# Last layer of a three-layer graph attention kernel: slots dealt anew to the engines, scores earlier in a period, own rows of the second layer weighted by ScalarE, last bias at other places

## The chip, the cores and the metric

The kernel runs on one core of one Trainium2 chip, as one launch. A core has TensorE (PE, matrix multiply, with its weight loads shown apart as PEld), VectorE (DVE), ScalarE (ACT), GpSimd (POOL) and SyncE (SP, which here only issues DMAs). Each engine takes its own instructions in order, and semaphores tie them together. The metric is the device time in microseconds (us).

## The reference, cut to what matters

The graph has 3125 nodes of 256 features and 53125 edges, sorted by destination. Three attention layers run one after the other (4 heads, 1 head, 8 heads). The first two are one residual block with a layer norm behind it, the third is the other:

```python
def gat_layer(x, src, dst, W, a_src, a_dst, bias, heads, out_ch):      # layers 1 and 2; in both, every
    xW = (x @ W).reshape(n, heads, out_ch)                             # node also has an edge to itself
    e = leaky_relu(sum(xW * a_src)[src] + sum(xW * a_dst)[dst], 0.2)
    w = exp(e - segment_max(e, dst)[dst])
    alpha = w / segment_sum(w, dst)[dst]
    return segment_sum(xW[src] * alpha[:, :, None], dst).reshape(n, heads * out_ch) + bias
...
    # layer 3, h = x @ W.T
    enc = relu(edge_attr @ edge_W.T + edge_b).reshape(-1, H, D)
    alpha = einsum(h[src], a_src) + einsum(h[dst], a_dst) + sum(enc * h[dst], axis=-1)
    # then leaky_relu, softmax over the edges of a destination, weighted sum of h[src], + bias
...
x = layernorm(x + L0(x)); x = layernorm(x + L1(x))
```

## The kernel before, in words

**Tiling.** The nodes lie in 25 blocks of 128 partitions (`nodes`). The edges are cut into slots of 128 edges that all end in one block, 440 slots, handled in `K` = 40 batches of `B` = 11 slots. A layer (index l = 0, 1, 2) first projects all blocks and writes a table of rows to memory, then runs 40 periods, one for each batch. In a period, slot s of the batch t is weighted (each of its 128 gathered rows times its edge weights, in place in `rows`), multiplied on PE with a matrix of zeros and ones that adds the rows of one destination (`sum_slot`, L1658), and the product is added to the sums of its block by DVE (`add`, L826). The sums stand in only two PSUM banks in the last layer, so the matmul of slot s waits for the add of slot s - 2.

**Who weights a slot.** `OWNER` is a string for each layer: V for DVE (one TENSOR_TENSOR, L815), A for ACT (one ACTIVATE for each head, L1414, 8 in the last layer), P for POOL (one TENSOR_TENSOR, L1237). DVE and ACT do it `LEAD[l]` positions ahead of the slot's matmul, two in the last layer: at position s they weight slot s + 2 of t, or, from position 9 on, slot 0 or 1 of the next batch.

**Beside it, each engine prepares the batches to come.** `n1`, `n2`, `n3` are the batches one, two, three later; `AT[l]` is a table that gives the position at which each small step is written. In the last layer DVE runs, in this order: `rescale` (L807) at the start of a period, `links` at 2, `finish_tops` (L779 to L787) at 5, `hot` (L707) at 7, `scores` of n2 (L717, L722) at 8, `tops` (L739, L745) and `tops2` (L753) at 10. Between them stand the dot products of encoded edge features with destination rows, in six groups a batch (`dot` L835, `dot2` L844), each after PE's `encode` (L1670, L1677) and ACT's `encode` (L1422). Batch k + 3 is encoded in period k, so the last three periods have none. ACT runs beside its weightings and encodings: `hotT` (L1366) at 2 and 5, `link` and `rescale` (L1382 to L1393) at 3, `expw` (L1399) at 6, `weights` (L1407, which hands out the edge weights of n1) at 8, the copy of scores (L1373) at 9. PE runs the matmuls that feed all of these. A semaphore `w` counts `weights`, `wp` the transpose that it copies, `fac` the factor of `rescale`, `ad` the lookup that `scores` reduces.

**POOL** in a period weights its slots of t and then issues the 11 row gathers of batch t + 3 by indirect DMA (L1225), in three groups of 4, 4 and 3. A group waits until PE has used the same buffers in batch t, that is for the matmuls of slots 0 to 3, 4 to 7 and 8 to 10.

**Ends of a layer.** A node's own row (its edge to itself) is not gathered. In layers 0 and 1 POOL weights it (`self_mul`, L1242) and adds the sums to it (`self_add`, L1249), block by block, in four runs of blocks (`READY`) as soon as the sums of a run are complete and DVE has computed their denominators (`self_weights`, L571 to L576). Then DVE forms the residual (L611), statistics and norm, PE and ACT project. ACT's `deviation` (L1332, a square root) stands first in its work for the last layer. In the last layer the bias of the block (L851) is added to all 25 blocks: three ahead of the first scores, 11 in each of the periods with three and with two batches left.

## Time and profile before

| what | value |
|---|---|
| median of 3 runs | 2139.15 us (2136.64 to 2141.73) |
| profiled execution, its time | 2139.67 us |
| profiled execution, its span | 2137.9 us |
| around the span (time less span) | 1.8 us |
| last layer, its 40 periods | 1420.7 to about 2117 us of the span |
| busy over the span | PE 76%, DVE 76%, POOL 72%, ACT 57% |
| granted TensorE clock, mean | 0.854 of full speed |

The span is the time from the first to the last instruction on the core. The table is read by stages, since the four engines are bound by different things in each: the busy shares over the whole span hide that in the last layer one engine is at work nearly all the time. A line number (L826) is that of the kernel printed above.

### The profile page before, as it was taken

Reading aid. Unit: us, or ns where it says so; the run is one execution under the profiler, and the core shown is the slowest. Engines: PE = TensorE matmul, PEld = TensorE weight load, DVE = VectorE, ACT = ScalarE, POOL = GpSimd, SP = SyncE. Lnnn points to the kernel's source line nnn. Section 1 sums busy time; section 2 is a strip of 40 time slices with the busy share of each in tenths; the row PEclk is TensorE's granted clock in tenths of the full one; section 3 lists DMA queues with packets and bytes.
Section 4 is the critical chain, followed back from the end, with each engine's and each line's share of the span. In section 5 each row is a group of like instructions: output and inputs, shape, how many; then the busy total and the mean of one; then the engine's idle time right before and its main releaser. Section 6 shows DMA issues by size and latency. Waiting matters only on the chain. (4 is left out here: it accounts for less than half of the span.)

```text
span 2137.9 us, 42617 instructions
## 1 busy us (share of the span) xinstructions
PE 1634.7 (76%) x9240; PEld 1035.0 (48%) x9240; DVE 1618.8 (76%) x4473; ACT 1219.4 (57%) x4310; POOL 1547.9 (72%) x1714
## 2 busy tenths in 40 slices
PE   6378778877774667777778776688998999989984
PEld 5245545555552434444445444345555555555552
DVE  5567777777678556666666667869999999999998
ACT  4257766676663445554555553546666666666655
POOL 3767777777778277777777777567788877878863
PEclk9577877787887778888887797879999999999995
DMA  6744554445640344444444641243444444444421
GB/s 197 177 136 141 141 142 141 137 142 157 187 121 30 95 128 136 135 136 135 136 129 134 197 122 39 89 125 112 126 137 131 127 125 127 130 131 132 134 75 60
DMA packets 131326, 274.35 MB, mean 128 GB/s; under 512 B 40389, under 2 KB 65968, under 8 KB 131061
## 3 DMA queue, kind: packets, MB, share of 16 engines
q0 software_dynamic: 64128, 181.33, 30.8%
q1 hardware_dynamic: 62259, 86.45, 13.3%
q10 hardware_dynamic: 4699, 3.86, 0.6%
q8 instruction: 92, 1.51, 0.3%
q14 instruction: 148, 1.21, 0.2%
HBM read 255.34 MB, written 17.20 MB: 127 GB/s over the span
## 5 line engine op out<-in xcount | busy, mean ns | idle before, releaser
L1225 POOL DMA_INDIRECT rows<-table,index_all x1320 | 1280.7, 970 | 478.6 <-issue 351.6
L1658 PE MATMUL bank<-rows,onehot 128*128 128x264 f32 (+1 forms) x2640 | 957.5, 473 | 167.4 <-ACT rows L1414 113.2
L826 DVE TENSOR_TENSOR sums<-sums,bank 128x264 f32 (+1 forms) x1320 | 554.8, 420 | 234.6 <-PE bank L1658 111.7
L1414 ACT ACTIVATE rows<-rows,wgt 128x65 f32<-128x65 f32 (+2 forms) x2480 | 664.1, 352 | 0.1
L1658 PEld LDWEIGHTS bank<-rows,onehot 128*128 128x128 f32 x2640 | 496.6, 222 | 339.5 <-ACT rows L1414 155.3
L1422 ACT ACTIVATE prod<-bank 128x512 f32<-128x512 f32 x240 | 134.9, 562 | 204.3 <-PE bank L1670 181.4
L1366 ACT CAST onehot<-bank 128x768 f32<-128x768 bf16 x240 | 175.3, 740 | 128.5 <-PE bank L1581 128.0
L1677 PE MATMUL bank<-late,onehotT 128*128 x1320 | 193.2, 282 | 0.7 <-DVE prod L835 0.7
L1373 ACT COPY scoreT<-bank 44x256 f32<-44x256 f32 (+2 forms) x120 | 39.6, 330 | 263.2 <-PE bank L1611 210.5
L835 DVE TENSOR_TENSOR prod<-prod,bank 128x512 f32<-128x512 f32 x240 | 151.7, 632 | 11.1 <-PE bank L1677 6.6
L1581 PE MATMUL bank<-identb,onehotT 128*128 128x128 bf16 x1320 | 143.6, 258 | 11.7 <-DVE onehotT L707 6.9
L844 DVE TENSOR_REDUCE dots<-prod 128x16 f32<-128x512 f32 x240 | 151.4, 631 | 0.5
L815 DVE TENSOR_TENSOR rows<-rows,wgt 128x260 f32<-128x260 f32 (+2 forms) x320 | 149.2, 467 | 0.7 <-ACT wgt L1407 0.6
L1677 PEld LDWEIGHTS bank<-late,onehotT 128*128 128x128 bf16 x1320 | 112.2, 100 | 62.4 <-issue 45.8
L1237 POOL TENSOR_TENSOR rows<-rows,wgt 128x264 f32<-128x264 f32 x200 | 129.1, 672 | 6.0 <-ACT wgt L1407 5.4
L1581 PEld LDWEIGHTS bank<-identb,onehotT 128*128 128x128 bf16 x1320 | 108.3, 117 | 44.2 <-issue 23.8
L1611 PE MATMUL bank<-ident,score 128*44 128x128 f32 (+1 forms) x160 | 39.1, 336 | 116.7 <-DVE score L729 113.9
L1594 PE MATMUL bank<-dtab,onehotT 128*128 x1320 | 104.3, 178 | 10.9 <-issue 10.3
L1594 PEld LDWEIGHTS bank<-dtab,onehotT 128*128 128x128 bf16 x1320 | 86.1, 97 | 43.1 <-issue 12.3
L1670 PE MATMUL bank<-edgew,late 30*128 30x256 bf16 x440 | 91.2, 280 | 9.2 <-DVE onehotT L707 8.5
L1564 PE MATMUL bank<-wts,rows 128*128 128x264 f32 (+2 forms) x300 | 87.0, 416 | 2.6 <-ACT rows L1313 2.6
L1399 ACT ACTIVATE expT<-expT 44x256 f32<-44x256 f32 (+2 forms) x120 | 45.5, 379 | 72.3 <-DVE expT L787 68.8
(200 smaller groups left out, 1787.6 us busy)
## 6 DMA issues: line engine op xcount, KB each, us to landing
locb<-loc_d SPq DMA_DIRECT2D x120, 352.0 KB, 3.7
rows<-table,index_all POOLq DMA_INDIRECT x1320
flags<-flags_d SPq DMA_DIRECT2D x520, 27.5 KB
table<-rows SPq DMA_DIRECT2D x25, 136.0 KB, 1.8
table<-rows SPq DMA_DIRECT2D x25, 134.0 KB, 3.1
late<-table SPq DMA_DIRECT2D x1, 3300.0 KB, 17.2
table<-rows SPq DMA_DIRECT2D x25, 129.5 KB, 2.0
late<-table SPq DMA_DIRECT2D x1, 3212.5 KB, 16.6
```

Of the source, the lines that this page charges most:

```text
L815: done(v.tensor_tensor(r, r, w.to_broadcast([P, H, n]), ALU.mult), "mulv")
L826: done(v.tensor_tensor(a, a, sum_bank(l, t, s)[:, 0:VV], ALU.add), "add")
L835: done(v.tensor_tensor(prod[:, i % 2, 0:w], prod[:, i % 2, 0:w], ps_hdst[i % 2][:, 0:w], ALU.mult), "prod")
L844: done(v.tensor_reduce(dots[:, t.u, :, lo:hi].rearrange("p h s -> p s h"), prod[:, i % 2, 0:(hi - lo) * D].rearrange("p (s h c) -> p s h c ...
L1225: g.indirect_dma_start(out=rows[:, t.u, s, 0:ROW[l]], out_offset=None, in_=table[l], in_offset=bass.IndirectOffsetOnAxis(ap=index_all[:, t ...
L1366: done(a.copy(onehot[:, t.u, lo:hi, :].rearrange("p s e -> p (s e)"), ps_hotb[l][g][:, 0:(hi - lo) * P]), "hotT")
L1414: i = a.activation(r, r, ACT.Copy, scale=wgt[:, t.u, h * B + s:h * B + s + 1])
L1422: done(a.activation(prod[:, i % 2, 0:w], ps_enc[:, 0:w], ACT.Relu), "enc")
L1581: r = m.transpose(ps_hotb[l][g][:, (s - lo) * P:(s - lo + 1) * P], onehotT[:, t.u, s * P:(s + 1) * P], identb[:, :])
L1594: r = m.matmul(ps_e[:, AD + s * 24:AD + (s + 1) * 24], onehotT[:, t.u, s * P:(s + 1) * P], dtab3[:, bass.ds(b, 1), :, :].rearrange("p a i ...
L1658: done(m.matmul(sum_bank(l, t, s)[:, 0:VV], onehot[:, t.u, s, :], rows[:, t.u, s, 0:VV], start=True, stop=True), "agg")
L1677: r = m.matmul(ps_hdst[i % 2][:, (s - lo) * D:(s - lo + 1) * D], onehotT[:, t.u, s * P:(s + 1) * P], hnode3[:, bass.ds(b, 1), j, :].rearra ...
```

## The change

It has five parts. (1) `OWNER` of the last layer: DVE has slots 0 and 2 (before 0, 1, 3), ACT 1, 3, 5, 7, 9 (before 2, 5, 8), POOL 4, 6, 8, 10 (before 4, 6, 7, 9, 10). (2) In the last layer `scores` of n2 stands at position 5 for DVE and its transpose at 8 for PE (before 8 and 9), the second `hot` of PE at 5 and `hotT` of ACT at 6 (before 4 and 5); DVE's scores no longer wait for `w` of n1 but for its `fac`, and PE's transpose of the weights of n1 waits for those scores. (3) Own rows of layer 1 are weighted by ACT (`self_scale`), one a slot in the last period and 14 in a row behind it. (4) POOL only adds there. (5) Of the 25 bias additions of the last layer, 11 stand ahead of the first period, 11 in the period with three left, 3 in the next.

```diff
-OWNER = ("AVAAVAAVAAV", "VAAAAAAAAAA", "VVAVPAPPAPP")
+OWNER = ("AVAAVAAVAAV", "VAAAAAAAAAA", "VAVAPAPAPAP")
...
+BIASED = 11
...
-    dict(links=2, finish=5, mask=10, scores=8, tops=10, hot=7, load=7,
-         link=3, exp=6, weights=8, hotT=(2, 5), copy=9,
-         endsT=1, cols=4, weightsT=7, hotP=(1, 4), adst=3, scoresT=9),
+    dict(links=2, finish=5, mask=10, scores=5, tops=10, hot=7, load=7,
+         link=3, exp=6, weights=8, hotT=(2, 6), copy=9,
+         endsT=1, cols=4, weightsT=7, hotP=(1, 5), adst=3, scoresT=8),
...
                     need(dve, "scT", kk)
                     need(dve, "ad", kk + 1)
-                    need(dve, "w", kk)
+                    if l == 2 and t.k > 1:
+                        need(dve, "w", kk - 1)
+                        need(dve, "fac", kk)
+                    else:
+                        need(dve, "w", kk)
...
-                        if l == 2 and left in (2, 3) and BLOCKS - 2 * B + (3 - left) * B + s < BLOCKS:
-                            bias_add(BLOCKS - 2 * B + (3 - left) * B + s)
+                        if l == 2 and left in (2, 3) and BIASED + (3 - left) * B + s < BLOCKS:
+                            bias_add(BIASED + (3 - left) * B + s)
...
                     dots_of(t0, *range(G))
-                    for b in range(BLOCKS - 2 * B):
+                    for b in range(0, 5):
                         bias_add(b)
-                    for f in (scores, tops, tops2):
-                        f(t0)
-                    dots_of(t1, 0, 1)
+                    scores(t0)
+                    for b in range(5, 7):
+                        bias_add(b)
+                    tops(t0)
+                    tops2(t0)
+                    dots_of(t1, 0)
+                    for b in range(7, 9):
+                        bias_add(b)
+                    dots_of(t1, 1)
                     links(t0)
+                    for b in range(9, BIASED):
+                        bias_add(b)
...
                     for b in READY[i]:
-                        self_mul(b)
-                        if b > READY[i][0]:
-                            self_add(b - 1)
-                    self_add(READY[i][-1])
+                        if l == 0:
+                            self_mul(b)
+                            if b > READY[i][0]:
+                                self_add(b - 1)
+                        else:
+                            self_add(b)
+                    if l == 0:
+                        self_add(READY[i][-1])
...
+                        if l == 1 and left == 1:
+                            self_scale(s)
+
+                def self_scale(b):
+
+                    for i, r in enumerate(READY):
+                        if b == r[0]:
+                            need(act, "selfq", NR + i + 1)
+                    if b == 0:
+                        act.wait_ge(s_self[1], 16)
+                    done(a.activation(selfs[1][:, b, 0:D], selfs[1][:, b, 0:D], ACT.Copy, scale=qz[:, 0, b, 0:1]), "selfx")
...
                 batches(act, period)
+                if l == 1:
+                    for b in range(B, BLOCKS):
+                        self_scale(b)
...
                     need_apart(pe, ("exp", kk + 1), ("w", kk))
+                    if l == 2 and 0 < t.k < K - 1:
+                        need(pe, "sc1", kk + 2)
```

Where it moves instructions, the engines' programs read as follows.

DVE from position 10 of one period to position 1 of the next, in the steady part of the last layer, before (L815 weights a slot, L807 starts a period, L826 adds a slot):

```order
L815 TENSOR_TENSOR rows<-rows,wgt 128x264 [waits ev_w]
L835 TENSOR_TENSOR prod<-prod,bank 128x256 [waits ev_encp,ev_enc]
L826 ISA [waits ev_add,ev_agg]
L826 TENSOR_TENSOR sums<-sums,bank 128x264
L753 SCALAR_TENSOR_TENSOR top<-flags,top 88x128 [waits ev_endp,ev_topf]
L844 TENSOR_REDUCE dots<-prod 128x8 [waits ev_prod]
L805 ISA [waits ev_w,ev_add,ev_fac,ev_ad]
L807 TENSOR_TENSOR sums<-sums,bank 128x264
L826 ISA [waits ev_resc,ev_agg]
L826 TENSOR_TENSOR sums<-sums,bank 128x264
L815 TENSOR_TENSOR rows<-rows,wgt 128x264 [waits ev_w]
L835 TENSOR_TENSOR prod<-prod,bank 128x512 [waits ev_encp,ev_enc]
```

and in the changed kernel (its lines are some five further down: L820 for L815, L812 for L807, L831 for L826):

```order
L840 TENSOR_TENSOR prod<-prod,bank 128x256 [waits ev_encp,ev_enc]
L831 ISA [waits ev_add,ev_agg]
L831 TENSOR_TENSOR sums<-sums,bank 128x264
L758 SCALAR_TENSOR_TENSOR top<-flags,top 88x128 [waits ev_endp,ev_topf]
L849 TENSOR_REDUCE dots<-prod 128x8 [waits ev_prod]
L810 ISA [waits ev_w,ev_add,ev_fac,ev_ad]
L812 TENSOR_TENSOR sums<-sums,bank 128x264
L820 TENSOR_TENSOR rows<-rows,wgt 128x264 [waits ev_w]
L831 ISA [waits ev_resc,ev_agg]
L831 TENSOR_TENSOR sums<-sums,bank 128x264
L840 TENSOR_TENSOR prod<-prod,bank 128x512 [waits ev_encp,ev_enc]
```

The weighting at position 10 is gone, and the one at position 1 stands ahead of the period's first add, between that add and the rescale that it waits for.

ACT from position 3 to position 0 of the next period, in the same part, before (L1422 encodes, L1414 weights a slot, L1366 is `hotT`, L1399 the exponential, L1407 hands out the weights, L1373 copies the scores):

```order
L1414 ACTIVATE rows<-rows,wgt 128x33 x8
L1422 ACTIVATE prod<-bank 128x512
L1366 CAST onehot<-bank 128x640
L1399 ACTIVATE expT<-expT 88x128
L1422 ACTIVATE prod<-bank 128x512
L1414 ACTIVATE rows<-rows,wgt 128x33 x8
L1407 COPY wgt<-bank 128x88
L1422 ACTIVATE prod<-bank 128x512
L1373 COPY scoreT<-bank 88x128
L1422 ACTIVATE prod<-bank 128x256
L1422 ACTIVATE prod<-bank 128x512
```

and in the changed kernel (some 17 lines further down: L1431 for L1414, L1439 for L1422):

```order
L1431 ACTIVATE rows<-rows,wgt 128x33 x8
L1439 ACTIVATE prod<-bank 128x512
L1431 ACTIVATE rows<-rows,wgt 128x33 x8
L1416 ACTIVATE expT<-expT 88x128
L1439 ACTIVATE prod<-bank 128x512
L1383 CAST onehot<-bank 128x640
L1431 ACTIVATE rows<-rows,wgt 128x33 x8
L1424 COPY wgt<-bank 128x88
L1439 ACTIVATE prod<-bank 128x512
L1390 COPY scoreT<-bank 88x128
L1439 ACTIVATE prod<-bank 128x256
L1431 ACTIVATE rows<-rows,wgt 128x33 x8
```

One weighting of eight ACTIVATEs (slot 7) now stands between the encode at position 4 and the exponential, one (slot 1 of the next batch) between the encode at 9 and the next period's first; the cast of `hotT` moved behind the encode at 6.

ACT at the end of layer 1, where its last weightings are followed by the square root of the layer norm, before:

```order
L1407 COPY wgt<-bank 128x11
L1414 ACTIVATE rows<-rows,wgt 128x257 x12
L1332 ACT_TABLE_LOAD
L1332 ACTIVATE rstd<-meanvar,eps 128x2 x2
L1313 COPY rows<-bank 128x256
```

and in the changed kernel, from the last of its weightings on (L1474 is `self_scale`; seven more stand between weightings ahead of this piece):

```order
L1431 ACTIVATE rows<-rows,wgt 128x257
L1474 ACTIVATE late<-late,qzr 128x256
L1431 ACTIVATE rows<-rows,wgt 128x257
L1474 ACTIVATE late<-late,qzr 128x256 x17
L1349 ACT_TABLE_LOAD
L1349 ACTIVATE rstd<-meanvar,eps 128x2 x2
```

The table load and the first square roots now stand behind the weighting of the last own row.

## Rows read from the trace of the kernel before

**Rows 1.** Windows, steady periods: length, busy us by engine, PEclk, DMA share, GB/s.
```profile
1482.70:2049.10 566.40, 510.42 (x3401) 317.23 (x3400) 533.59 (x1288) 368.52 (x1289) 452.50 (x529) 1.00 0.45 129
```
**Rows 2.** Timeline of DVE: starts of period 1 and of the third last.
```profile
1447.52 0.42 DVE L807 TENSOR_TENSOR sums<-sums,bank 128x264 f32 x1
...
2066.62 0.41 DVE L807 TENSOR_TENSOR sums<-sums,bank 128x264 f32 x1
```
**Rows 3.** Timeline of DVE, one period: start us, us, instruction [idle before <-releaser].
```profile
1604.03 0.42 DVE L807 TENSOR_TENSOR sums<-sums,bank 128x264 f32 x1
1604.65 0.43 DVE L826 TENSOR_TENSOR sums<-sums,bank 128x264 f32 x1 [0.21 <-DVE sums L807]
1605.00 0.73 DVE L815 TENSOR_TENSOR rows<-rows,wgt 128x264 f32<-128x264 f32 x1
1605.65 0.68 DVE L835 TENSOR_TENSOR prod<-prod,bank 128x512 f32<-128x512 f32 x1
...
1615.83 0.42 DVE L717 TENSOR_REDUCE adsum<-bank 128x88 f32<-128x264 f32 x1
...
1619.44 0.40 DVE L815 TENSOR_TENSOR rows<-rows,wgt 128x264 f32<-128x264 f32 x1
1619.76 0.41 DVE L835 TENSOR_TENSOR prod<-prod,bank 128x256 f32<-128x256 f32 x1
...
1621.08 0.41 DVE L807 TENSOR_TENSOR sums<-sums,bank 128x264 f32 x1
```
**Rows 4.** Timeline of POOL, the same period: weightings, then first gathers of two groups.
```profile
1605.42 3.17 POOL L1237 TENSOR_TENSOR rows<-rows,wgt 128x264 f32<-128x264 f32 x5
...
1608.87 0.98 POOL L1225 DMA_INDIRECT rows<-table,index_all  x1 [0.27 <-PE bank L1658]
...
1613.99 0.95 POOL L1225 DMA_INDIRECT rows<-table,index_all  x1 [0.38 <-PE bank L1658]
```
**Rows 5.** Timeline of ACT, the same period: what it waits for.
```profile
1606.27 0.60 ACT L1422 ACTIVATE prod<-bank 128x512 f32<-128x512 f32 x1 [1.14 <-PE bank L1670]
...
1610.96 0.69 ACT L1366 CAST onehot<-bank 128x640 f32<-128x640 bf16 x1
1611.76 0.31 ACT L1399 ACTIVATE expT<-expT 88x128 f32<-88x128 f32 x1
1612.44 0.60 ACT L1422 ACTIVATE prod<-bank 128x512 f32<-128x512 f32 x1 [0.37 <-PE bank L1670]
1612.93 1.80 ACT L1414 ACTIVATE rows<-rows,wgt 128x33 f32<-128x33 f32 x8
1614.63 0.21 ACT L1407 COPY wgt<-bank 128x88 f32<-128x88 f32 x1
1615.85 0.60 ACT L1422 ACTIVATE prod<-bank 128x512 f32<-128x512 f32 x1 [1.01 <-issue]
1617.15 0.26 ACT L1373 COPY scoreT<-bank 88x128 f32<-88x128 f32 x1 [0.70 <-issue]
...
1619.89 0.60 ACT L1422 ACTIVATE prod<-bank 128x512 f32<-128x512 f32 x1 [1.70 <-PE bank L1670]
```
**Rows 6.** Timeline, end of layer 1: POOL, ACT and DVE.
```profile
1296.91 1.23 POOL L1242 TENSOR_TENSOR late<-late,qzr 128x256 f32<-128x256 f32 x2 [12.21 <-DVE qzr L571]
...
1300.71 4.92 ACT L1414 ACTIVATE rows<-rows,wgt 128x257 f32<-128x257 f32 x12
1310.34 1.28 ACT L1332 ACT_TABLE_LOAD   x1 [4.71 <-DVE meanvar L552]
...
1321.50 0.28 DVE L571 SCALAR_TENSOR_TENSOR qzr<-sums 128x5 f32<-128x5 f32 x1
...
1322.72 0.17 DVE L559 RECIPROCAL rstd<-rstd 128x2 f32<-128x2 f32 x1
```
**Rows 7.** Timeline of DVE, ahead of the first period of the last layer.
```profile
1392.37 1.08 DVE L851 TENSOR_TENSOR nodes<-nodes,bias 128x256 f32<-128x256 f32 x3
...
1396.03 0.31 DVE L722 TENSOR_TENSOR score<-rows,adsum 128x88 f32<-128x88 f32 x1 [2.23 <-DMA rows<-table,index_all]
```

More of the change, by code:

```diff
@@ L283, in gat_kernel @@
             "h1 h2 h3 "
-            "selfq selfz selfr selfm selfa e5 e6 e7 ex e8 "
+            "selfq selfz selfr selfm selfx selfa e5 e6 e7 ex e8 "
             "self2 sum stat aggr std rst shf scl norm norm2").split()
@@ L1245, in self_add @@
                 def self_add(b, l=l):
-                    need(pool, "selfm", l * BLOCKS + b + 1)
+                    need(pool, ("selfm", "selfx")[l], b + 1)
                     t = own(l, b)
@@ L1298, in _ @@
             fetch(1)
-            seeded(act, "link hotT scp rrise rscale exp w mula enc yT tval ex h2 std norm2")
+            seeded(act, "link hotT scp rrise rscale exp w mula enc yT tval ex h2 std norm2 selfx")
             for l in range(3):
```

## The prediction

> **What bounds the kernel now.** I read the windows of the busy engines over a stretch of the last layer first, then the timeline of one period there, engine by engine, and then the two ends of the layer. In the steady stretch DVE is busy 533.6 of 566.4 us, which is 94%, PE 90%, POOL 80%, ACT 65%, at a granted clock of 1.00 [rows 1]. POOL's 80% deceives: the 0.27 to 0.30 us ahead of each gather is not counted as busy but is spent all the same [rows 4]. One period lasts 17.05 us, from 1604.03 to 1621.08 [rows 3], and the 36 periods from 1447.52 to 2066.62 take 619.1 us, 17.20 each [rows 2], so disturbed ones add 0.15 on average. In the clean period DVE has one wait of 0.21 us for its own rescale [rows 3] and goes from instruction to instruction otherwise. POOL goes round in the same 17.05 us: 3.17 us of weightings, then 11 gathers, and its wait before the second group is 0.38 us where 0.30 is there anyway, so only about 0.08 us is slack [rows 4]. Two engines are thus full, DVE and POOL; ACT has some 6 us idle in a period (17.2 less 65%), nearly all of it ahead of encodings and the copy of scores: 1.14, 0.37, 1.01, 0.70, 1.70 [rows 5].
>
> **DVE in a period.** It loses the weighting at position 10, which takes 0.32 us from its start to the next one's, and the one at position 1, which takes 0.65 [rows 3]. It gets one at position 0, between the rescale and the first add, where now 0.62 us pass with 0.21 of them idle [rows 3]. Rescale and weighting follow each other at some 0.34, so the first add would start at 0.68 instead of 0.62: 0.06 more. Sum: -0.65 - 0.32 + 0.06 = -0.91, so 16.14 us. This counts on the new weighting taking the short time (0.40 to the end), not the long one (0.73). The long one starts at 1605.00 and POOL's weightings at 1605.42; the other ones on DVE, away from those, take 0.40 [rows 3, 4]. At position 0 it would run from about 1604.37 and be over before POOL starts. The other end of the range is that it stays at 0.65: 16.14 + 0.31 = 16.45.
>
> Here the Trainium skill has a rule (SBUF — State Buffer, section "Who interferes with whom"): a VectorE instruction with two SBUF inputs and a GpSimd one that reads SBUF exclude each other, and the later one blocks until the first ends. The trace shows the slowdown in that pair but not that order: the DVE instruction was first by 0.42 us and was still the long one. Taken to the letter, its 0.31 us would have another cause and stay, and DVE's sum would be 16.45 instead of 16.14, which is the end of the range that the rows gave too.
>
> **POOL in a period.** Five weightings of 3.17 us become four, -0.63; with the 0.08 of slack gone the loop is 17.05 - 0.08 - 0.63 = 16.34 us [rows 4]. That is more than DVE's 16.14, so POOL is the next bound. Its gathers are released by PE's matmuls of slots 3, 7 and 10, which now also wait for ACT.
>
> **ACT in a period.** A weighted slot is eight ACTIVATEs of 1.70 us from start to the next instruction [rows 5], and it gets two more: +3.4 us. I let the idle time carry them. Slot 1 of the next batch stands ahead of the first encoding of the period, where ACT idles 1.70 us: it fits. Slot 7 stands ahead of the exponential in the place of the cast of 0.69 us, so the exponential comes 1.70 - 0.69 = 1.0 us later than at 1611.76, the encoding behind it (0.37 idle) 0.7 later, and the weights (1614.63) 1.3 later, since slot 9 and the cast stand ahead of them as well; the waits behind, 1.01 and 0.70, take that up [rows 5]. Who waits for the late ones: PE's transpose of the weights, with the matmuls of slots 7 and 8 queued behind it, for the exponential; DVE's weighting of slot 0 of the next batch at position 9 for the weights. Before, the scores at position 8 waited for these weights as well; now they stand at 5 (L717, 0.42 [rows 3]) and wait only for the factor, which is why the delay doesn't reach them. Their own time is unchanged and the lookups and gathered rows that they need are there earlier. The later cast and the earlier transposes of PE are moved within its queue, at no cost as long as PE's 10% idle covers them [rows 1]; the cost if it doesn't is the transpose's delay itself, up to 1.0 us a period. Total ACT: 65% of 17.05 is 11.1, with 3.4 it is 14.5 of 16.34. I take 0.1 us a period for waits that this tightness brings, between 0 and the 0.91 that would eat DVE's gain.
>
> A rule of the Trainium skill speaks against the change (ScalarE: Activation LUTs, section "Rules for kernel authors"): multiplications belong on VectorE, not ScalarE. The rows agree on the price, 1.70 us on ACT against 0.32 to 0.65 on DVE and 0.63 on POOL. If the engine's time were what counts, 2 x 1.70 x 36 = 122 us would be lost; what counts is whether it was idle, and the sum above needs only that.
>
> **Steady part.** Period 16.34 + 0.15 (disturbances as before) + 0.1 = 16.6 against 17.20: -0.6, times 36 = **-21.6 us**. The ends: 16.34 with nothing added, -0.86 x 36 = -31; no gain, 0.
>
> **The first period and what lies ahead.** Eight more bias additions of some 0.36 us (1.08 us for three) stand in DVE's waits ahead of the first period; the one for gathered rows alone is 2.23 us for the first four of them [rows 7]. Free; 8 x 0.36 = 2.9 if none of it were. But ACT weights slot 1 of batch 0 (1.70) ahead of its last two encodings where DVE took 0.4: I take +0.8, between 0 and 1.7, less 0.4 inside the first period, where two weightings of DVE go as well: +0.4.
>
> **The last periods.** With three batches left DVE loses the same two weightings, -0.9. With two left it also loses eight bias additions, 8 x 0.36 = 2.9, part of which waits for PE will swallow: -2.3 (between 0 and -2.9), to which the weightings add nothing that I count.
>
> **End of layer 1.** POOL loses 25 weightings of some 0.6 us (1.23 for two) [rows 6], 15 us in all, which are now ACTIVATEs of about 0.41 (4.92 us for 12 of nearly that shape [rows 6]). POOL wasn't waited for there. But ACT's first square root, with its table load, moves behind the last own row: it needs the denominators of the last run, which begin at 1321.50, so 0.3 + 5 x 0.41 + 1.28 + 0.29 = 3.9 us later, at 1325.4, where DVE reads it at 1322.72 [rows 6]: +2.7. Against it, DVE's two-input instructions from 1297 to 1328 run beside a POOL that is busy half as long; nine residuals and the denominators there could gain 1 to 3 us. I take +0.6, between -2 and +3.
>
> **Sum.** -21.6 + 0.4 - 0.9 - 2.3 + 0.6 = -23.8. The profiled execution took 2139.67 us (span 2137.9 and 1.8 around it): 2115.9; the median of the runs is 0.5 lower, so **2115.4 us**.
>
> **The rivals.** (a) *ACT becomes the pacing engine*, half covered: the late exponential and weights hold up the transpose on PE or the weighting at position 9 on DVE by some 0.35 us in each period. For it: they come 1.0 and 1.3 us late and the waits meant to absorb that are 2.1 us in all; against: PE had been standing idle for ACT in just that part. Period 16.95, -0.25 x 36 = -9, less 2.2 for the ends: 2128. (b) *The waits of ACT don't shrink*: an encoding waits for a matmul that follows slots weighted by ACT itself, so idle time may travel along with the work. If the 1.14, 0.37, 1.01 and 0.70 stayed [rows 5], the period would be 11.1 + 3.4 + 3.2 = 17.7, +0.5 x 36 = +18, less 2.2: 2155, slower. It decides from 2.7 us of kept waits a period (17.2 - 14.5). Against it: those waits are for PE matmuls that themselves hang on DVE's adds, and an engine that comes later meets them done. (c) *POOL alone sets the pace*, without the 0.1 and with fewer disturbances: -31 - 2.2 = 2106. (d) *DVE's weighting stays long* (the rule above taken to the letter): 16.45 + 0.25 = 16.7, -0.5 x 36 = -18, less 2.2: 2119.5, within the forecast's own range. (e) *It moves nothing*: DVE's gain eaten where POOL and PE release each other; then only the ends, 2137.
>
> **How the numbers follow.** Forecast with (d), 2107 to 2122: 62%, of which 12% are (d). (a), 2122 to 2133: 18%. (c), under 2107: 8%. (e): 4%. (b): 8%. The range from 2106 to 2131 leaves out (b), (e) and the outer parts of (a) and (c), some 18%. A measurement of this kernel tells about 0.2% (4.3 us) from no change: faster by more 89%, within it 4%, slower 7%.
>
> **What would show it.** Right: starts of the rescale 16.4 to 16.6 us apart; five groups of eight ACTIVATEs in a period of ACT, and its wait ahead of the first encoding gone; the DVE weighting behind the rescale at 0.4 us; POOL's loop without waits beyond 0.30; scores without a wait; the reading of the first square root at about 1323 to 1326. Wrong: DVE waiting at the product of the fourth group or at position 9 for ACT (a); ACT's waits ahead of encodings as long as before and PE waiting for rows of ACT more than now (b); the new weighting at 0.7 (d).

## The result

The changed kernel took 2128.5 us (median of 20 runs, 2116.8 to 2138.4) against 2140.9 us of the kernel before (median of 20 runs beside it): a ratio of 0.9939, interval 0.9925 to 0.9952. It is faster by 12 us where 24 were forecast. 2128.5 lies within the range on record (2106 to 2131), but at the number of rival (a), 2128, and not near the forecast of 2115. The profiled execution took 2125.35 us against 2139.67: 14.3 us less.

The starts of the rescale (now L812) say where. Before the last layer's first period the two traces stand at the same place (1420.73 before, 1420.84 after). The first period is 1.4 us shorter, the 36 steady ones 9.1 us together (619.1 to 610.0, that is 16.94 each in place of 17.20), the one with three batches left 1.3, the one with two left 2.3, what follows 0.4. So the steady part gave 9.1 us where 21.6 were forecast, and the ends together gave 5.2 us where 2.2 were forecast: the gap lies in the steady part alone, and is 12.5 us there. First the windows of the steady part of the changed kernel (columns as in [rows 1]) and, from the timelines of DVE, POOL and ACT, one of its short periods:

```profile
1482.80:2039.65 556.85, 523.77 (x3401) 332.21 (x3399) 514.38 (x1255) 463.45 (x1817) 435.67 (x495) 0.97 0.48 131
```

```profile
1701.68 0.42 DVE L812 TENSOR_TENSOR sums<-sums,bank 128x264 f32 x1
1702.02 0.42 DVE L820 TENSOR_TENSOR rows<-rows,wgt 128x264 f32<-128x264 f32 x1
1702.36 0.42 DVE L831 TENSOR_TENSOR sums<-sums,bank 128x264 f32 x1
...
1707.66 0.43 DVE L831 TENSOR_TENSOR sums<-sums,bank 128x264 f32 x1 [0.24 <-PE bank L1691]
...
1717.97 0.42 DVE L812 TENSOR_TENSOR sums<-sums,bank 128x264 f32 x1
```

```profile
1702.10 1.16 POOL L1238 DMA_INDIRECT rows<-table,index_all  x1 [0.30 <-issue]
1703.56 0.95 POOL L1238 DMA_INDIRECT rows<-table,index_all  x1 [0.30 <-issue]
1704.53 2.41 POOL L1250 TENSOR_TENSOR rows<-rows,wgt 128x264 f32<-128x264 f32 x4
...
1712.13 0.95 POOL L1238 DMA_INDIRECT rows<-table,index_all  x1 [0.30 <-issue]
```

```profile
1703.97 0.60 ACT L1439 ACTIVATE prod<-bank 128x512 f32<-128x512 f32 x1 [1.05 <-PE bank L1703]
...
1707.87 0.60 ACT L1439 ACTIVATE prod<-bank 128x512 f32<-128x512 f32 x1 [0.26 <-PE bank L1703]
...
1713.14 0.60 ACT L1439 ACTIVATE prod<-bank 128x512 f32<-128x512 f32 x1
...
1716.95 0.60 ACT L1439 ACTIVATE prod<-bank 128x512 f32<-128x512 f32 x1 [0.49 <-PE bank L1703]
```

This period takes 16.29 us and is the one that was worked out: the weighting behind the rescale takes 0.42, as forecast, and not the 0.73 of [rows 3]; four weightings on POOL take 2.41 in place of 3.17; POOL never stands for more than the 0.30 or 0.31 ahead of each gather and so is the bound, at 16.29 where the sum had said 16.34. ACT is 83% busy (463.45 of 556.85), and its waits have shrunk: the 1.14 of [rows 5] is 1.05, the 1.70 is 0.49, the 1.01 is gone. But the windows show a granted clock of 0.97 where [rows 1] have 1.00, and only some of the periods look like this one: 23 of the 36 take 16.3 to 16.7 us, the other 13 take 17.6 to 18.6, about 17.8 most of them.

One of the long ones runs from 1601.67 to 1619.43 (17.76 us). Windows of one microsecond in it, and then the timelines of PE, POOL and DVE:

```profile
1606.50:1607.50 1.00, 1.00 (x8) 0.63 (x7) 0.96 (x2) 1.00 (x6) 0.84 (x2) 1.00 0.00 0
1607.50:1608.50 1.00, 1.00 (x7) 0.59 (x7) 0.76 (x3) 0.69 (x3) 0.69 (x2) 0.68 0.00 0
1608.50:1609.50 1.00, 1.00 (x9) 0.80 (x8) 0.70 (x3) 1.00 (x7) 0.82 (x1) 0.50 0.50 139
...
1610.50:1611.50 1.00, 1.00 (x4) 0.38 (x3) 0.81 (x3) 0.00 (x0) 0.70 (x2) 0.62 0.57 151
1611.50:1612.50 1.00, 1.00 (x10) 0.73 (x10) 1.00 (x3) 0.61 (x2) 0.32 (x1) 1.00 0.61 200
```

```profile
1604.52 1.14 PE L1625 MATMUL bank<-dtab,onehotT 128*128 x11
1605.61 0.68 PE L1691 MATMUL bank<-rows,onehot 128*128 128x264 f32 x2
1606.22 0.47 PE L1662 MATMUL bank<-ones,linkrow 1*88 1x1 f32 x4
1606.55 0.36 PE L1671 MATMUL bank<-scale,carry 2*128 2x8 f32 x2
...
1607.81 1.45 PE L1710 MATMUL bank<-late,onehotT 128*128 x6
1609.06 0.74 PE L1612 MATMUL bank<-identb,onehotT 128*128 128x128 bf16 x5
1609.59 1.94 PE L1691 MATMUL bank<-rows,onehot 128*128 128x264 f32 x4
```

```profile
1613.44 0.94 POOL L1238 DMA_INDIRECT rows<-table,index_all  x1 [1.63 <-PE bank L1691]
```

```profile
1614.32 0.43 DVE L831 TENSOR_TENSOR sums<-sums,bank 128x264 f32 x1 [0.92 <-issue]
```

The clock granted to PE goes from its upper level (2.4 GHz) to the lower (1.2 GHz) at about 1608 and comes back at about 1611. In between the six matmuls of L1710 take 1.45 us instead of 0.83, and four of the sums' 1.94 instead of 1.11. POOL's second group of gathers, released by the sum of slot 7, waits 1.63 instead of 0.30, DVE's next add waits 0.92, and the period ends 1.47 us late (17.76 less 16.29). PE wasn't idle in the 4 us before the fall: the rows show it busy all through, but with the work that stands at positions 3 and 4, part of which is narrow, that is, has few columns for each matmul (eleven matmuls of 24 columns in L1625, then columns of 1 and of 8 in L1662 and L1671). The change took five transposes of 128 columns (L1612, the second group of `hot`) out of just that stretch. By the granted clock, the 36 steady periods of the changed kernel hold 13 stretches at the lower level, some 45 us in all. Twelve are of this sort: they begin 5.3 to 6.6 us into a period, with no wait of PE in the 3 us ahead of them. The first of the 13 is another sort: it begins at the end of the first period, behind waits of PE of 1.3 us together. The kernel before holds one such stretch, of 3 us, 6.4 us into its period.

### The profile page after: what moved, and what is told of

Its sections match the earlier page's. It is cut to its first block and busy times, and to the rows that moved or that the text cites. A ratio compares the mean times of both kernels' runs of the same rounds, so it can differ in the third digit from the quotient of the medians.

```text
span 2123.5 us, 43220 instructions
## 1 busy us (share of the span) xinstructions
PE 1636.8 (77%) x9240; PEld 1044.7 (49%) x9240; DVE 1592.1 (75%) x4433; ACT 1345.7 (63%) x4975; POOL 1507.5 (71%) x1649
## 3 DMA queue, kind: packets, MB, share of 16 engines
q14 instruction: 152, 1.25, 0.2%
HBM read 255.34 MB, written 17.20 MB: 128 GB/s over the span
## 5 line engine op out<-in xcount | busy, mean ns | idle before, releaser
L1431 ACT ACTIVATE rows<-rows,wgt 128x33 f32<-128x33 f32 (+2 forms) x3120 | 809.0, 344 | 0.2
L831 DVE TENSOR_TENSOR sums<-sums,bank 128x264 f32 (+1 forms) x1320 | 554.8, 420 | 239.4 <-PE bank L1691 134.3
L1439 ACT ACTIVATE prod<-bank 128x512 f32<-128x512 f32 x240 | 134.2, 559 | 124.5 <-PE bank L1703 116.2
L1710 PE MATMUL bank<-late,onehotT 128*128 x1320 | 198.9, 288 | 0.4 <-DVE prod L840 0.4
L1612 PE MATMUL bank<-identb,onehotT 128*128 128x128 bf16 x1320 | 145.0, 259 | 11.6 <-DVE onehotT L708 6.5
L1710 PEld LDWEIGHTS bank<-late,onehotT 128*128 128x128 bf16 x1320 | 114.1, 101 | 63.8 <-issue 45.3
L1612 PEld LDWEIGHTS bank<-identb,onehotT 128*128 128x128 bf16 x1320 | 113.0, 119 | 45.0 <-issue 24.3
L820 DVE TENSOR_TENSOR rows<-rows,wgt 128x260 f32<-128x260 f32 (+2 forms) x280 | 120.7, 431 | 0.7 <-ACT wgt L1424 0.6
L1625 PE MATMUL bank<-dtab,onehotT 128*128 x1320 | 104.5, 178 | 11.0 <-issue 10.0
L1625 PEld LDWEIGHTS bank<-dtab,onehotT 128*128 128x128 bf16 x1320 | 86.2, 97 | 43.7 <-issue 13.3
L1250 POOL TENSOR_TENSOR rows<-rows,wgt 128x264 f32<-128x264 f32 x160 | 98.3, 649 | 4.7 <-ACT wgt L1424 4.1
L1642 PEld LDWEIGHTS bank<-ident,score 128*44 128x44 f32 (+1 forms) x160 | 10.6, 104 | 155.8 <-DVE score L734 152.7
## 6 DMA issues: line engine op xcount, KB each, us to landing
late<-table SPq DMA_DIRECT2D x1, 3212.5 KB, 17.8
```

The source lines that it names most:

```text
L831: done(v.tensor_tensor(a, a, sum_bank(l, t, s)[:, 0:VV], ALU.add), "add")
L1431: i = a.activation(r, r, ACT.Copy, scale=wgt[:, t.u, h * B + s:h * B + s + 1])
L1439: done(a.activation(prod[:, i % 2, 0:w], ps_enc[:, 0:w], ACT.Relu), "enc")
L1612: r = m.transpose(ps_hotb[l][g][:, (s - lo) * P:(s - lo + 1) * P], onehotT[:, t.u, s * P:(s + 1) * P], identb[:, :])
L1625: r = m.matmul(ps_e[:, AD + s * 24:AD + (s + 1) * 24], onehotT[:, t.u, s * P:(s + 1) * P], dtab3[:, bass.ds(b, 1), :, :].rearrange("p a i ...
L1710: r = m.matmul(ps_hdst[i % 2][:, (s - lo) * D:(s - lo + 1) * D], onehotT[:, t.u, s * P:(s + 1) * P], hnode3[:, bass.ds(b, 1), j, :].rearra ...
```

## The experiments

Two theories stood against each other. **Theory 1**: the moved transposes leave a stretch of PE too thin, and the clock falls there. **Theory 2**: the shorter period alone brings the falls. In two of the four groups of runs, among them the first, everything waited longer: the kernel before took 2556 and 2579 us where it takes 2140. In the kernel before with only the transposes moved, a gather still took 970 ns there and an add 421 in place of 420, but the steady periods were 19.5 to 23.1 us and the clock in them 0.88. The groups are told apart below by the time of the kernel before. Ratios are compared inside a group, or between the two groups in which the kernel before took 2140 (2140.4 in that of the control, 2139.8 in the other). The changed kernel itself was not run in the groups at 2556 and 2579.

**The changed kernel again**, as a control (kernel before 2140):

> The changed kernel as it is, as a control beside the four runs ahead, in which the kernel before took 2556 us where it had taken 2140: PE stood for 1 to 4 us at a time in the middle of a period, for something that the profile doesn't name, and periods were 20.0 to 21.9 us. If those waits hold the periods whatever the owners, the changed kernel is within 0.3% of the kernel before here; if its gain is independent of them, the ratio is 0.994 as in the first comparison. Theory 1 (moved transposes) wants it above e1_hot_back, 0.9877, by 0.005 or more; theory 2 wants the two within 0.002.

2124.5 us, ratio 0.9934 (0.9914 to 0.9954). The trace shows 13 stretches at the lower clock again, some 45 us in all, the same twelve and one, and 610.2 us for the 36 periods, nearly to the decimal what the first trace had. Many of them come some 34 us apart, one in every second period (1468, 1502, 1536, 1570, 1605), which is a short and a long period together. The ratio is 0.0057 above that of the kernel of the next section in the group at 2556, as theory 1 wanted, but that comparison crosses into a group where everything waited, and shows nothing.

**The transposes back at position 4:**

```diff
-         endsT=1, cols=4, weightsT=7, hotP=(1, 5), adst=3, scoresT=8),
+         endsT=1, cols=4, weightsT=7, hotP=(1, 4), adst=3, scoresT=8),
```

> The changed kernel with one number set back: PE's second group of five transposes of the last layer (hot, slots 6 to 10) again at position 4 of the period, where it stood before, in place of 5. The changed kernel showed 11 stretches of some 3 us with the granted clock at 0.5 in the steady part, each following the narrow matmuls (24 columns) of positions 3 and 4, and each costing its period about 1.45 us. Theory 1, the moved transposes opened that gap: the stretches go, all periods are 16.3 to 16.4, and the time is 10 to 16 us below the changed kernel (2113 to 2119). Theory 2, the shorter period alone brings them, wherever the transposes stand: 8 to 14 of them stay and the time is within 3 us of the changed kernel's 2128.

> The same kernel as e1_hot_back (the changed kernel, PE's second group of five transposes of the last layer at position 4 again), repeated because in the first group of runs everything waited longer, the kernel before as well. Theory 1 (the moved transposes open a gap in PE's work, in which the clock falls): the stretches at 0.5 in the steady part go from 10 or so to at most 3, periods are 16.3 to 16.4, and the ratio to the kernel before is 0.986 to 0.989. Theory 2 (the shorter period alone brings them): 8 to 14 of them stay and the ratio is 0.993 to 0.995, that of the changed kernel.

In the first group (before 2556) 2525.7, ratio 0.9877 (0.9859 to 0.9895), which says nothing of the theories without the changed kernel beside it. Repeated (before 2140): 2120.6 us, ratio 0.9909 (0.9889 to 0.9929), neither the 0.986 to 0.989 of theory 1 nor the 0.993 and more of theory 2. The trace resolves it: the stretches go from 13 to 4 (three behind the narrow work, and the one at the end of the first period), as theory 1 wants, but the periods without one now average 16.69 us, not 16.42. In the timelines of DVE and POOL:

```profile
1672.09 0.43 DVE L831 TENSOR_TENSOR sums<-sums,bank 128x264 f32 x1 [0.84 <-PE bank L1691]
```

```profile
1676.27 1.15 POOL L1238 DMA_INDIRECT rows<-table,index_all  x1 [0.63 <-PE bank L1691]
```

In the changed kernel the same batch (its period of 16.69 us from 1668.70) has these instead:

```profile
1675.08 0.43 DVE L831 TENSOR_TENSOR sums<-sums,bank 128x264 f32 x1 [0.60 <-PE bank L1691]
```

```profile
1679.26 1.15 POOL L1238 DMA_INDIRECT rows<-table,index_all  x1 [0.40 <-PE bank L1691]
```

The waits are 0.24 and 0.23 us shorter there, and so is the period (16.69 against 16.92). In most other batches DVE's wait is 0.48 against 0.24. At position 4 the transposes delay the sum that DVE's next add waits for, and with it the slot 7 on which POOL waits. There POOL's wait is longer by less than 0.1 us, but its gather then starts beside DVE's `hot` (L708) and takes 1.15 us in place of 0.95: 26 such gathers in the 36 periods, against 2 in the control. Moving them away, as the change does, gains 0.27 us a period on average (10 us in 36) and costs nine falls. By the lengths of the periods, the 13 falls of the control cost 19 us and the four here 4.5, so the falls cost more than the place gains, and the difference is the 4.7 us between 610.2 and 605.4 us for the 36 periods.

**The same move alone, in the kernel before:**

```diff
-    dict(links=2, finish=5, mask=10, scores=8, tops=10, hot=7, load=7,
-         link=3, exp=6, weights=8, hotT=(2, 5), copy=9,
-         endsT=1, cols=4, weightsT=7, hotP=(1, 4), adst=3, scoresT=9),
+    dict(links=2, finish=5, mask=10, scores=8, tops=10, hot=7, load=7,
+         link=3, exp=6, weights=8, hotT=(2, 6), copy=9,
+         endsT=1, cols=4, weightsT=7, hotP=(1, 5), adst=3, scoresT=9),
```

> The kernel before with only PE's second group of transposes moved from position 4 to 5 and the cast behind it on ACT from 5 to 6; owners of the weightings, scores, own rows and biases as before. Theory 1 (the moved transposes open the gap in PE's wide work): several stretches at clock 0.5 in the steady part, up to one in each third period, and the time 5 to 20 us above the kernel before. Theory 2 (only the shorter period brings them): at most one or two such stretches, period 17.0 to 17.2, and the time within 3 us of the kernel before.

> The same kernel as e2_hot_alone (the kernel before with only those transposes and the cast behind them one position later), repeated for the same reason. Theory 1: several stretches at clock 0.5 in the steady part, the ratio to the kernel before 1.002 to 1.01. Theory 2: at most two of them, ratio 0.999 to 1.001. The disturbed group of runs gave 0.9993.

First group: ratio 0.9993 (0.9981 to 1.0004). Repeated (before 2140): 2144.3 us, ratio 1.0016 (1.0004 to 1.0028), three stretches against one, and 625.1 us for the 36 periods against 619.1:

```profile
1446.45:2071.56 625.11, 562.56 (x3706) 350.60 (x3704) 582.23 (x1404) 402.49 (x1412) 487.57 (x573) 0.99 0.46 126
```

The sign is that of theory 1, the number of falls nearer to theory 2. So the place of the transposes does it only in part; at a period of 17.1 us they bring two more falls, at 16.3 nine. Two more falls rest on one trace of each kernel. What else in the change brings falls, the shorter period or the other moves on PE, was not taken apart.

**Work added in the thin stretch of the changed kernel:**

```diff
                         r = m.matmul(ps_e[:, AD + s * 24:AD + (s + 1) * 24], onehotT[:, t.u, s * P:(s + 1) * P],
...
                                      start=True, stop=True)
+                        if l == 2 and s % 2:
+                            m.matmul(ps_e[:, QT:QT + 8 * B], identb[:, :], identb[:, 0:8 * B], start=True, stop=True)
                     done(r, "ad")
```

> The changed kernel with work added: behind every second of the 11 narrow matmuls (24 columns) of position 3 in the last layer PE does one more matmul, of 88 columns in bf16, into unused columns, five a period, some 0.2 us of PE in sum by the matmul rates of the trace; nobody reads them. Theory 1 (the clock falls because PE's work in positions 3 and 4 is thin): fewer stretches at 0.5, fewer than 5 of the 11, and the time 5 to 15 us below the changed kernel in spite of the added work. Rival (the falls have to do with something else, such as waits of PE in the whole period): as many stretches as without, and the time 0 to 7 us above the changed kernel.

> The same kernel as e4_filler (the changed kernel with five more matmuls of 88 columns a period among the narrow ones of position 3), repeated for the same reason. If the clock falls because PE's work is thin there: at most 4 stretches at 0.5 in the steady part, periods of 16.3 to 16.5, ratio to the kernel before 0.985 to 0.989, below the changed kernel's 0.993. If the falls come from elsewhere: 8 or more, ratio 0.993 to 0.997.

First group: 2511.7, ratio 0.983 (0.9814 to 0.9847). Repeated (before 2140): **2110.7 us, ratio 0.9859** (0.9839 to 0.988), better than both kernels. Windows over the same 36 periods, of the changed kernel's control, of the transposes at 4, and of this one:

```profile
1442.87:2053.04 610.17, 573.15 (x3710) 363.10 (x3708) 560.89 (x1369) 506.99 (x1989) 472.34 (x536) 0.96 0.47 129
```

```profile
1446.50:2051.93 605.43, 561.77 (x3707) 351.46 (x3704) 560.40 (x1369) 506.35 (x1989) 476.93 (x536) 0.99 0.48 130
```

```profile
1443.66:2037.33 593.67, 556.75 (x3890) 355.72 (x3888) 559.56 (x1369) 505.65 (x1989) 471.79 (x536) 1.00 0.49 132
```

PE does 180 matmuls more and is busy 16.4 us less. DVE, ACT and POOL are busy for the same time in the first and the third to within 1.4 us, and the clock is 1.00: one stretch is left, at the start. The 36 periods take 593.7 us, 16.5 less than in the control, with 12 stretches fewer: 1.4 us each. This is the run that settles what held the gain back: nothing but PE's own work at position 3 was changed, the falls behind the narrow work went, and the steady part is 25.4 us shorter than before where 21.6 had been forecast.

PE's idle time doesn't explain the falls. This is the kernel before over its 36 periods:

```profile
1447.52:2066.62 619.10, 556.27 (x3706) 345.75 (x3704) 581.81 (x1405) 403.24 (x1412) 491.07 (x573) 1.00 0.45 127
```

| kernel, groups at 2140 | PE idle a period | falls behind narrow work |
|---|---|---|
| before | 1.75 us | 1 |
| before, transposes at 5 | 1.74 us | 3 |
| changed | 1.03 us | 12 |
| changed, transposes at 4 | 1.21 us | 3 |
| changed, work added at 3 | 1.03 us | 0 |

The idle time is the length less PE's busy time in the windows, divided by 36. The kernel with most of it has one fall, and two with the same idle time have twelve and none.

**Is it the place, or any work?** In the last group (before 2579) the five matmuls stood at position 7, ahead of the transpose of the weights:

```diff
                         need(pe, "sc1", kk + 2)
+                        for _ in range(5):
+                            m.matmul(ps_e[:, QT:QT + 8 * B], identb[:, :], identb[:, 0:8 * B], start=True, stop=True)
                     m_ = m.transpose(ps_e[:, WT:WT + H * B], expT[0:H * B, 0, :], ident[0:H * B, 0:H * B])
```

> The changed kernel with the same five matmuls of 88 columns, but at position 7, ahead of the transpose of the weights, where PE's work is wide on both sides. If the clock falls for the thin stretch at positions 3 and 4: as many stretches at 0.5 as in the changed kernel (8 to 12 in the steady part), ratio to the kernel before 0.992 to 0.995. Rival, what counts is PE's work over the whole period, wherever it stands: at most 4 of them, ratio 0.985 to 0.989.

2543.4 us, ratio 0.986 (0.9844 to 0.9876). That is the number of the rival, but the trace has 20 stretches in the steady part, and the two kernels with the work at position 3 had 24 (first group) and 26 (next but one, same group) under such conditions. All 20 stand behind a wait of PE, so they are of another sort than those in question: with PE standing in each period for something else, falls come whatever is added. The changed kernel wasn't run in this group; the nearest one without added work, the last layer's owners and positions alone, has 0.9873, and the two intervals overlap. This stays open: that the added work must stand in the thin stretch isn't shown.

**The same work in the kernel before** (same lines, before 2579):

> The kernel before with the same five added matmuls of 88 columns a period as e4b_filler, among the narrow ones of position 3. There the steady part had one stretch at 0.5. If the added work gives only what the falls of the clock cost, it has 1.5 to 3 us to give here: ratio 0.998 to 1.000. Rival: the added matmuls help in another way too (they warm or reorder something for all periods); then a ratio near that of e4b_filler to the changed kernel, 0.993.

2577.9 us, ratio 0.9997 (0.9982 to 1.0011): no gain of its own, as expected of work that nobody reads, though this group can't show the 1.5 us of the one fall either, and its trace has 36 falls of the other sort.

**The last layer's owners and positions alone**, the own rows of layer 1 back on POOL and the last bias where it was (first and last group):

```diff
-BIASED = 11
+BIASED = BLOCKS - 2 * B
...
-                    need(pool, ("selfm", "selfx")[l], b + 1)
+                    need(pool, "selfm", l * BLOCKS + b + 1)
```

> The changed kernel with two parts undone: the own rows of the second layer weighted by POOL again, and the last bias added where it was (3 additions ahead of the first period, 11 in each of the last-but-two and last-but-one). What is left is the last layer's new owners and positions. By the ledger of the two traces the moved bias gave 2.3 us and the own rows +0.2: this kernel should be 2 to 3 us slower than the changed one, 2130 to 2131, ratio to the kernel before 0.995. Rival: the own rows cost more than the ledger shows, 2 us or so hidden in the shift between layers; then it equals the changed kernel.

> The same kernel as e3_periods_alone (own rows of the second layer and the last bias as in the kernel before, only the last layer's owners and positions changed), repeated since everything waited longer in that group of runs. By the ledger: 2 to 3 us slower than the changed kernel, ratio 0.9945 to 0.9955; the rescale of the last-but-one period some 2.3 us longer after the one before, the shift between layers 0.2 us shorter. Rival: the own rows on ACT cost 2 us or more there; then the ratio is 0.993 or lower.

2521.7 us, ratio 0.9863 (0.9846 to 0.988), and 2546.9 us, ratio 0.9873 (0.9856 to 0.989): not to be told from 0.9877 and 0.986 of kernels with those parts in the same groups. Those two aren't the changed kernel (one has the transposes at 4, the other the added work), so the expected 2 to 3 us is neither met nor refuted. The traces say more. The period with two batches left takes 16.2 us in both, against 13.7 to 14.9 in the three others of these groups with the bias moved: 1.3 to 2.5 us for that part. And from layer 1's last rescale but one to the last layer's first one it is 128.3 us in the kernel before and 128.5 with only the transposes moved, but 128.9, 130.2, 130.4 and 130.2 in the four undisturbed traces with the own rows on ACT. So own rows and early biases together cost 0.6 to 2.1 us there, and the moved bias gives about as much back in the late period (that the first comparison has the start of the last layer only 0.1 us later has an earlier part in it that varies from run to run). What waits at the end of layer 1 of the changed kernel (ACT, then DVE): ACT weights the last five own rows, loads its table, and DVE stands 3.42 us for the square root.

```profile
1320.15 2.11 ACT L1474 ACTIVATE late<-late,qzr 128x256 f32<-128x256 f32 x5 [7.08 <-DVE qzr L572]
1322.28 1.28 ACT L1349 ACT_TABLE_LOAD   x1
```

```profile
1323.97 0.17 DVE L560 RECIPROCAL rstd<-rstd 128x2 f32<-128x2 f32 x1 [3.42 <-ACT rstd L1349]
```

**More of it in the last two periods**, on top of the work at position 3:

```diff
+                            if left < 3 and 3 <= s < (7 if left == 2 else B):
+                                filler(t, s, left)
```

Ahead of the first of them PE also waits for the rescale, the weights and the scores (three `need` in `filler`), so this edit adds waits beside the matmuls.

> e4b_filler with more of the same in the last two periods, where the narrow matmuls of position 3 are no longer there: five matmuls of 88 columns ahead of each slot from 3 to 6 with two batches left, and from 3 to 10 with one left. In e4b_filler the clock stood at 0.5 from 2038 to 2052 and one of the late periods took 16.6 us where the changed kernel had 14.6. If PE sets those periods: 1 to 3 us below e4b_filler, 2108 to 2110, ratio 0.984 to 0.986. Rival: DVE with its adds and biases sets them, or the fillers are too few to raise the clock; no difference within 1.5 us.

2542.3 us, ratio 0.9857 (0.9842 to 0.9873), beside 0.983 of the kernel without it in the first group. Its last two periods before the final one take 18.1 and 12.8 us, 31.0 together, where the kernel without that work had 17.8 and 14.0 (first group) and the one with the work at position 7 16.1 and 13.7. In such a group 1 to 3 us can't be told; whether the tail has something to give is open.

## Why the prediction was half right

- **POOL's sum** held to a few hundredths, in part by luck. The short periods take 16.29 us against 16.34, and POOL is the bound. But its four weightings take 2.41 where the sum had 2.54, the wait behind them is 0.16 instead of 0.27, and against that the gather that starts beside DVE's moved weighting (1702.10, 0.08 us behind it) takes 1.16 where the others take 0.95. That happens in 35 of the 36 periods (1.16 to 1.44 us), and raises the mean of all gathers in them from 0.958 to 0.982 us, which is 0.26 a period of the engine that is the bound. No term stood for it, and no run moves the weighting away from the gather.
- **DVE's sum** of 16.14 was high: in the short period DVE waits 0.20 and 0.24 us for PE, so its own work takes at most some 15.9. One reason is in the period that the sum started from, where DVE had a second wait of 0.20 (at 1614.89) beside the one of 0.21. The weighting behind the rescale takes 0.42, so rival (d) fell. The operation has the same shape and operands as the one of 0.73, and is short when POOL isn't weighting beside it. So POOL's weightings were what made it long, though they had started 0.42 us later, and that is not the order that the Trainium skill gives (SBUF — State Buffer, "Who interferes with whom"). A gather of POOL ran until 1605.40 as well, but DVE's weighting at 1616.91 of the same period ran beside a gather and took 0.43.
- **ACT's idle time carried the new work**, and rivals (a) and (b) fell. Its waits of 0.37, 1.01 and 0.70 [rows 5] are gone, and in the steady part PE no longer waits for rows of ACT. The exponential comes 0.66 us later in its period than before and the weights 0.75, where 1.0 and 1.3 had been taken, and nothing stands for them. Before (35.1 us in 33 waits) and after, PE's largest waits there are:

```profile
PE bank L1658 <- ACT rows L1414: 35.1, 33, 1.1
```

```profile
PE bank L1691 <- DVE sums L831: 24.1, 37, 0.8
PE bank L1651 <- DVE top L758: 6.4, 28, 0.3
```

  The 0.1 us a period that the sum allowed for tightness wasn't needed: with the work added on PE and the clock held, the 36 periods averaged 16.49, which is 16.34 + 0.15. That it fits to the digit is chance, since POOL's loop is 16.29 and the 0.20 above it is made of other things than the 0.15 was.
- **The step that failed** is "0.15 (disturbances as before)", with its neighbour, that moving PE's transposes is "at no cost as long as PE's 10% idle covers them". The 0.15 was carried over as if it could not change. Of its 5.3 us in 36 periods, 1.7 were one fall of the clock: a period of 18.77 us from 1499.87, with the clock at 0.5 from about 1506 to 1510, which wasn't asked after. In the changed kernel that part grew: the period averages 16.94 where the undisturbed one takes 16.29, so the term is 0.65 and not 0.15 or, with the 0.1, 0.25. Of the 0.65, 0.5 are the 13 falls, which lengthen their periods by 1.4 us and more, 19 us in all. The price that was named for the move, a delay of the transpose, doesn't occur in the short periods; the price that occurs wasn't among the rivals. That the result landed at rival (a)'s 2128 is chance, since its mechanism is absent.
- **The late periods** came out, 1.3 and 2.3 us shorter against 0.9 and 2.3. The first period gave more than it should, 1.4 where 0.4 had been taken. The additions ahead of it are mostly hidden: DVE still waits for gathered rows behind the first five.

```profile
1390.88 1.78 DVE L856 TENSOR_TENSOR nodes<-nodes,bias 128x256 f32<-128x256 f32 x5
...
1395.43 0.31 DVE L727 TENSOR_TENSOR score<-rows,adsum 128x88 f32<-128x88 f32 x1 [2.42 <-DMA rows<-table,index_all]
```

- **End of layer 1**: the +2.7 us of the square root came out. On the clock of the span DVE reads it only 1.25 us later (1323.97 against 1322.72), but layer 1 had ended 1.5 us earlier. Its last rescale, before and after:

```profile
1305.51 0.42 DVE L807 TENSOR_TENSOR sums<-sums,bank 128x258 f32 x1
```

```profile
1304.03 0.42 DVE L812 TENSOR_TENSOR sums<-sums,bank 128x258 f32 x1
```

  From it to the reading it is 17.21 us before and 19.94 after. The other traces agree: 17.2 in all with the own rows on POOL, 19.9 to 20.5 in all with them on ACT. The last denominators begin 15.99 and 15.92 us behind it, so nothing was gained there. The gain from less of POOL's work beside DVE is real but stands earlier: layer 1's last period takes 13.1 to 13.6 us with the own rows on POOL and 12.1 to 12.3 with them on ACT, 1.0 less where 1 to 3 had been expected (2.1 were taken). The stretch with what lies ahead of the first period was put at +0.6 and +0.8; it is +0.6 in the first trace and about +2 in three others.

## What to carry to other kernels

Ahead of moving anything on an engine with a clock that depends on its activity, look at the clock in windows of a microsecond and ask what the engine does in the stretch that loses work; busy shares don't tell it, since PE was fully busy in that stretch before and after. When a shorter period brings less than its undisturbed instances promise, list the periods one by one before looking at waits: two lengths (16.3 and 17.8) say more than their mean (16.9). And a useless matmul of 0.04 us, five times a period, may be the cheapest cure: it gave 14 us here, in the kernel that had the falls.

## What the runs showed of the hardware

- PE's clock fell from its upper to its lower level without a gap in PE's rows: in 12 of the 13 falls of the changed kernel, 5.3 to 6.6 us into a period, behind eleven matmuls of 24 columns and a few of 1 and 8. The Trainium skill (TensorE: Matmul & The Clock Gate, section "HAM oscillation — how this bites in real kernels") describes the clock as lost in waits for DMA, in which PE stands idle. These falls differ: the windows ahead of the one shown have PE busy 1.00 of 1.00. Others in these traces do stand behind a wait of PE, all 20 of the kernel with the work at position 7 among them. That the narrowness is what counts fits the runs in the groups at 2140, but the counts of columns weren't varied by themselves.
- A fall lasted 3.4 us, and cost the period 1.4 us in the changed kernel, 1.2 with the transposes at 4, and 1.6 and 1.8 in the two kernels with the old owners. In the long period shown, POOL's wait of 1.63 instead of 0.30 makes up 1.33 of it.
- A gather on POOL that started within some 0.1 us of DVE's weighting of 128x264 took 1.16 to 1.44 us in place of 0.95. The second weighting of a period starts 0.3 to 0.5 us ahead of its gather, and that gather takes 0.95 in most periods.
- A kernel's scatter can tell of it: runs of the changed kernel spread over 22 us, those of the kernel before over 12, and those with the added work over 4 (but only four of them).
- In two groups of runs all kernels were about 20% slower, with the instructions of DVE, ACT and POOL unchanged; one wait in such a group, from its timeline of DVE (work added at position 7), is put down to no engine of the core:

```profile
1850.94 0.43 DVE L831 TENSOR_TENSOR sums<-sums,bank 128x264 f32 x1 [1.71 <-remote]
```

  What the engines waited for there stays open.
